# Shared expert of a decoder layer on one NeuronCore: split fp32r products with the weights stationary, two tiles of tokens at a time

## What is computed

```python
x = x + attention(layernorm(x))              # 32 heads, 8 kv heads, rope, sinks
x = x + cross_attention(layernorm(x), ctx)   # 8 heads
x = x + ffn(layernorm(x))

def ffn(h):                                  # 8 experts, top 1, 512 inner units
    logits = h @ router_w.T
    xr = h * sigmoid(logits of the chosen expert, -inf elsewhere)
    routed = (up * silu(gate)) @ down_proj[expert]
    shared = silu(h @ shared_gate_w) * (h @ shared_up_w) @ shared_down_w
    return shared + routed
```

## Time and profile before

| what | value |
|---|---|
| median of 3 runs | 2001.04 us (1997.6 to 2002.55) |
| the profiled execution's own time | 1998.05 us |
| its span in the profile | 1996.2 us |
| attention, about | to 954 us |
| cross-attention and router, about | 960 to 1554 us |
| first gate matmul of the shared tiles | 1557.25 us |
| first gate matmul of the routed tiles | 1750.52 us |
| mean granted clock of TensorE, share of full speed | 0.959 |

### The profile page before, as it was taken

One profiled execution on the slowest core, in us unless ns is written; L12 is line 12 of the kernel. 1 busy time (PEld: TensorE's weight loads), 2 busy tenths in 40 slices (PEclk: granted clock), 3 DMA queues, 4 the chain that ended last, 5 costly groups with the idle time before them and its releaser, 6 DMA issues. The chain is left out here.

```text
span 1996.2 us, 44689 instructions
## 1 busy us (share of the span) xinstructions
PE 1806.2 (90%) x14992; PEld 1378.2 (69%) x14993; DVE 1156.6 (58%) x2205; ACT 797.6 (40%) x1495; POOL 809.3 (41%) x1280
## 2 busy tenths in 40 slices
PE   3999999999999999998699999999996799999997
PEld 2777777877787778776576776676773456666664
DVE  5776677666766676765666666676772222222222
ACT  3333443344333434343266666666663111111111
POOL 3545455545554555443323333333333100034443
PEclk9999999999999999998688989999997899999999
DMA  5011111111111111112333433443431282222221
GB/s 174 16 52 54 42 43 47 53 47 41 43 53 50 42 39 53 53 35 56 102 93 87 106 98 106 106 106 101 108 96 56 76 296 71 66 66 67 64 67 39
DMA packets 142007, 148.33 MB, mean 74 GB/s; under 512 B 26962, under 2 KB 136598, under 8 KB 140154
## 3 DMA queue, kind: packets, MB, share of 16 engines
q1 hardware_dynamic: 136186, 133.46, 24.0%
q0 software_dynamic: 5760, 14.06, 2.2%
HBM read 93.46 MB, written 54.11 MB: 74 GB/s over the span
## 5 line engine op out<-in xcount | busy, mean ns | idle before, releaser
L1129 DVE TENSOR_REDUCE xmax<-bankX 128x4 f32<-128x1024 f32 x256 | 310.1, 1217 | 155.2 <-PE bankX L1214 153.6
L1084 ACT ACTIVATE xe<-bankXT 128x512 f32<-128x512 f32 x512 | 293.2, 597 | 128.6 <-PE bankXT L1225 113.9
L1225 PE MATMUL bankXT<-stq,stk 98*128 98x256 f32 x1024 | 236.7, 319 | 31.8 <-DMA stq<-sh 26.3
L369 POOL TENSOR_TENSOR roped<-ropeC,ropeD 128x512 f32<-128x512 f32 x160 | 205.8, 1292 | 57.1 <-DVE ropeD L530 57.1
L1225 PEld LDWEIGHTS bankXT<-stq,stk 98*128 98x128 f32 x1024 | 163.8, 201 | 70.0 <-ACT xe L1084 47.5
L557 DVE TENSOR_TENSOR oTl<-bankV,oTh 128x512 fp32r<-128x512 f32 x128 | 88.1, 688 | 199.4 <-ACT oTh L445 199.4
L1540 DVE TENSOR_TENSOR hid<-bankU,gate 128x512 f32<-128x512 f32 x72 | 49.8, 692 | 246.3 <-PE bankU L1593 240.0
L1214 PE MATMUL bankX<-stk,stq 96*128 96x256 f32 x1024 | 179.2, 301 | 13.7 <-DMA rw<-in_rw 11.1
L662 PE MATMUL bankQ<-wqh,xnTh 128*128 128x512 f32 x384 | 189.5, 493 | 0.0
L1486 ACT ACTIVATE gate<-bankG 128x512 f32<-128x512 f32 x72 | 43.0, 597 | 347.0 <-PE bankG L1593 347.0
L1214 PEld LDWEIGHTS bankX<-stk,stq 96*128 96x128 f32 x1024 | 153.0, 206 | 16.8 <-DMA rw<-in_rw 11.3
(11 more groups left out here) (175 smaller groups left out, 3755.0 us busy)
## 6 DMA issues: line engine op xcount, KB each, us to landing
stackk_d<-chl SPq DMA_DIRECT2D x96, 128.0 KB, 2.3
stackq_d<-q2hl SPq DMA_DIRECT2D x96, 128.0 KB, 2.3
stk<-stackk_d SPq DMA_DIRECT2D x32, 384.0 KB
stq<-stackq_d SPq DMA_DIRECT2D x128, 96.0 KB
wexp<-in_wexp SPq DMA_DIRECT2D x8, 1536.0 KB, 8.4
x_d<-x SPq DMA_DIRECT2D x64, 128.0 KB, 1.8
xrden<-inv_d SPq DMA_DIRECT2D x64, 128.0 KB, 2.5
xin<-xg_d SPq DMA_DIRECT2D x40, 128.5 KB, 2.1
```

The costliest lines, as they stand in the source:

```text
L369: nc.gpsimd.tensor_tensor(roped[c % 3][:], ropeC[c % 2][:], ropeD[c % 2][:], ALU.add).then_inc(s_rsum, 1)
L1084: nc.scalar.activation(xe[q][:].rearrange("p n m -> p (n m)"), bT[:, q % 2, :], ACT.Exp).then_inc(s_xe, 1)
L1129: nc.vector.tensor_reduce(xmax[tile[1] % 2][:, :, a:b + 1:b - a].rearrange("p m h -> p h m"), bS[:, 2 * (pr % 2):2 * (pr % 2) + 2, :].rear ...
L1225: ins = nc.tensor.matmul(bT[:, q % 2, n * D:(n + 1) * D], stk[p][0:98, hd // 4, n * P:(n + 1) * P], stq[p][0:98, hd, :], start=True, stop= ...
```

## The change

The shared expert becomes a pipeline of its own, ahead of the routed tiles. It runs over 16 groups of two tiles (256 tokens, `g`) and, in each, 4 units of 128 inner units (`n` counts all 64).

- `up_s`: 128 columns of the gate (or up) weights are stationary, `[128 features, 128 inner units]`, and the 256 tokens move; the result has the inner units on partitions. Every product is three fp32r products of the high and low parts, so 6 matmuls of 256 columns for gate and 6 for up.
- ScalarE applies silu to the gate, VectorE multiplies, ScalarE copies the high part `hsh`, VectorE subtracts to `hsl`. No transposes and no `hT` copy remain.
- `down_s`: `hsh` and `hsl` of 128 tokens are stationary, 256 columns of down weights move, 6 matmuls per unit.
- The rows must come in turned. The router's stage has them turned already (xn3T), so `cross` now stores xn3T (`xn3T_d`, 512 bytes in a row) in place of xn3. SP's store of x2 moves up behind `s_x2`, the wait for `s_norm` goes, the store of xn3T stands at the end of the tile's queue, and `xa` now waits for `s_f3` also. The ScalarE copy to xn3T waits for the store of the tile before.
- The shared weights are split once, by GpSimd in tiles 1 to 3 of `cross`, from `wraw` into `wshh` and `wshl`.
- The rows of a group are split as they arrive: ScalarE copies `xsh`, GpSimd subtracts `xsl`.
- The base row x2 is loaded, added to and stored for two tiles at a time (`xb`).
- SP loads one expert's weights in each of groups 1 to 8. The table goes out and in again in group 3.
- The routed pipeline starts when the last shared unit is through.

```diff
-                    sp.wait_ge(s_norm, at(y) + 1)
-                    sp.dma_start(G.xn3_d[bass.ds(at(y) * P, P), :], xn3[yp][:]).then_inc(s_fst[yp], 16)
+                    sp.wait_ge(s_x2, at(y) + 1)
                     sp.dma_start(G.x2_d[bass.ds(at(y) * P, P), :], x2[yp][:]).then_inc(s_fst[yp], 16)
...
+                    if five:
+                        sp.wait_ge(s_f3, at(y) + 1)
...
+                if five:
+                    if not three:
+                        sp.wait_ge(s_f3, at(y) + 1)
+                    sp.dma_start(G.xn3T_d[:, :, bass.ds(at(y) * P, P)].rearrange("k p n -> p k n"), xn3T[:]).then_inc(s_fst[y[1] % 2], 16)
...
-            sp.dma_start(G.wsh[:], A["wexp"][E]).then_inc(G.s_wsh, 16)
+            sp.dma_start(wraw[:], A["wexp"][E]).then_inc(G.s_wsh, 16)
...
+            def split_shared(i):
+                a, b = i * WE // 3, (i + 1) * WE // 3
+                if i == 0:
+                    pool.wait_ge(G.s_wsh, 16)
+                nc.gpsimd.tensor_copy(G.wshh[:, a:b], wraw[:, a:b]).then_inc(G.s_wshh, 1)
+                pool.wait_ge(G.s_wshh, 2 * i + 1)
+                nc.gpsimd.tensor_tensor(G.wshl[:, a:b], wraw[:, a:b], G.wshh[:, a:b].bitcast(F32),
+                                        ALU.subtract).then_inc(G.s_wshh, 1)
...
+                if not inside(tile) and 1 <= at(tile) < 4:
+                    split_shared(at(tile) - 1)
...
+                        o = prev(y, 1)
+                        need(act, s_fst[o[1] % 2], (pair(o) + 1) * 32)
...
+            def load_x(g):
+                need(sp, s_u, NF * (g - 1))
+                sp.dma_start(xs[g % 2][:], G.xn3T_d[:, :, g * 2 * P:(g + 1) * 2 * P].rearrange(
+                    "k p n -> p k n")).then_inc(s_xin[g % 2], 16)
+            def load_base(g):
+                need(sp, s_yst[g % 2], 16 * (g // 2))
+                sp.dma_start(xb[g % 2][:], x2_d[g * 2 * P:(g + 1) * 2 * P, :].rearrange(
+                    "(i p) d -> p i d", i=2)).then_inc(s_x2in[g % 2], 16)
+            def store(g):
+                sp.wait_ge(s_y, 2 * (g + 1))
+                sp.dma_start(base_d[g * 2 * P:(g + 1) * 2 * P, :].rearrange("(i p) d -> p i d", i=2),
+                             xb[g % 2][:]).then_inc(s_yst[g % 2], 16)
...
+            for g in range(2):
+                load_x(g)
+            for g in range(2):
+                load_base(g)
+            for g in range(1, NG + 1):
+                if 2 <= g + 1 < NG:
+                    load_x(g + 1)
+                store(g - 1)
+                if 2 <= g + 1 < NG:
+                    load_base(g + 1)
+                if g <= E:
+                    sp.dma_start(wexp[:, (g - 1) * WE:g * WE], A["wexp"][g - 1]).then_inc(s_w, 16)
...
+            def low_x(g):
+                pool.wait_ge(s_xsh, g + 1)
+                nc.gpsimd.tensor_tensor(xsl[g % 2][:], xs[g % 2][:], xsh[g % 2][:].bitcast(F32),
+                                        ALU.subtract).then_inc(s_xT, 1)
...
+            def high_x(g):
+                act.wait_ge(s_xin[g % 2], 16 * (g // 2 + 1))
+                nc.scalar.activation(xsh[g % 2][:], xs[g % 2][:], ACT.Copy).then_inc(s_xsh, 1)
+            def gate_s(n):
+                act.wait_ge(s_g, n + 1)
+                need(act, s_d, n - 1)
+                nc.scalar.activation(hs[n % 2][:], bk[n % 2][:, 0, 0:2 * P], ACT.Silu).then_inc(s_silu, 1)
+            def high_h(n):
+                act.wait_ge(s_h, n + 1)
+                nc.scalar.activation(hsh[n % 2][:], hs[n % 2][:], ACT.Copy).then_inc(s_th, 1)
...
+            high_x(0)
+            high_x(1)
+            for n in range(NS):
+                gate_s(n)
+                high_h(n)
+                if n % NF == 0 and 2 <= n // NF + 1 < NG:
+                    high_x(n // NF + 1)
...
+            def hidden_s(n):
+                dve.wait_ge(s_silu, n + 1)
+                dve.wait_ge(s_u, n + 1)
+                nc.vector.tensor_tensor(hs[n % 2][:], bS[:, n % 2, 0:2 * P], hs[n % 2][:], ALU.mult).then_inc(s_h, 1)
+            def low_h(n):
+                dve.wait_ge(s_th, n + 1)
+                nc.vector.tensor_tensor(hsl[n % 2][:], hs[n % 2][:], hsh[n % 2][:].bitcast(F32),
+                                        ALU.subtract).then_inc(s_hT, 1)
+            def result_s(g):
+                dve.wait_ge(s_d, NF * (g + 1))
+                dve.wait_ge(s_x2in[g % 2], 16 * (g // 2 + 1))
+                for i in range(2):
+                    nc.vector.tensor_tensor(xb[g % 2][:, i, :], xb[g % 2][:, i, :], bX[:, g % 2, i * D:(i + 1) * D],
+                                            ALU.add).then_inc(s_y, 1)
...
+            result_s(NG - 1)
...
+            def three(a, b):
+                return ((a[0], b[0]), (a[0], b[1]), (a[1], b[0]))
+            def up_s(n, half, out, done):
+                g, c = n // NF, n % NF
+                if half == 0:
+                    if c == 0:
+                        pe.wait_ge(s_xT, g + 1)
+                    need(pe, s_silu, n - 1)
+                else:
+                    need(pe, s_h, n - 1)
+                for k in range(2):
+                    at = (k * 2 + half) * FF + c * P
+                    for i, (w, x) in enumerate(three((wshh[:, at:at + P], wshl[:, at:at + P]),
+                                                     (xsh[g % 2][:, k, :], xsl[g % 2][:, k, :]))):
+                        ins = nc.tensor.matmul(out, w, x, start=(k == 0 and i == 0), stop=(k == 1 and i == 2))
+                ins.then_inc(done, 1)
+            def down_s(n):
+                g, c = n // NF, n % NF
+                pe.wait_ge(s_hT, n + 1)
+                if c == 0:
+                    need(pe, s_y, 2 * (g - 1))
+                at = 4 * FF + c * D
+                for j in range(2):
+                    for i, (x, w) in enumerate(three((hsh[n % 2][:, j * P:(j + 1) * P],
+                                                      hsl[n % 2][:, j * P:(j + 1) * P]),
+                                                     (wshh[:, at:at + D], wshl[:, at:at + D]))):
+                        ins = nc.tensor.matmul(bX[:, g % 2, j * D:(j + 1) * D], x, w, start=(c == 0 and j == 0 and i == 0),
+                                               stop=(c == NF - 1 and i == 2), skip_group_check=True)
+                ins.then_inc(s_d, 1)
...
+                up_s(n, 0, bk[n % 2][:, 0, 0:2 * P], s_g)
+                up_s(n, 1, bS[:, n % 2, 0:2 * P], s_u)
+                if n >= 1:
+                    down_s(n - 1)
             turn_in((0, 0))
-            seq(pe, body, EDGES)
+            down_s(NS - 1)
+            pe.wait_ge(s_tab, 16)
```

More of the change, by code:

```diff
@@ L76, in constants @@
     put("none", NTOK)
-    put("tile", p[:, None] - NTOK // P)
+    put("tile", p[:, None])
     return c
@@ L1344, in experts @@
         xin = [sb(f"xin{p}", [P, D + 1]) for p in range(2)]
+        xs = [sb(f"xs{p}", [P, 2, 2 * P]) for p in range(2)]
+        xsl = [sb(f"xsl{p}", [P, 2, 2 * P], F32R) for p in range(2)]
+        xsh = [sb(f"xsh{p}", [P, 2, 2 * P], F32R) for p in range(2)]
+        hs = [sb(f"hs{p}", [P, 2 * P]) for p in range(2)]
+        hsl = [sb(f"hsl{p}", [P, 2 * P], F32R) for p in range(2)]
+        hsh = [sb(f"hsh{p}", [P, 2 * P], F32R) for p in range(2)]
+        xb = [sb(f"xb{p}", [P, 2, D]) for p in range(2)]
         xT = [sb(f"xT{p}", [P, 2, P]) for p in range(2)]
@@ L1378, in _ @@
         def _(sp):
-            def row(tile):
-                return sp.value_load(tabr[0:1, bass.ds(num(tile) * 2, 1)], min_val=0, max_val=XROWS - P)
-            def load(tile, like):
-                h, p = tile
-                if like < NT + 2:
-                    need(sp, s_tx, num(tile) - 1)
-                else:
-                    sp.wait_ge(s_tok, num(tile) - NT - 1)
-                if like < NT:
-                    sp.dma_start(xin[p][:, 0:D], xn3_d[bass.ds(num(tile) * P, P), :]).then_inc(s_xin[p], 16)
-                else:
-                    if like == NT:
-                        sp.wait_ge(s_tab, 16)
-                        sp.wait_ge(s_padd, 16 * E)
-                        for q in range(2):
-                            sp.wait_ge(G.s_scat[q], 16 * (NT // 2))
-                    sp.dma_start(xin[p][:], xg_d[bass.ds(row(tile), P), :]).then_inc(s_xin[p], 16)
@@ new lines, in load_base, with load @@
+            def load_base(g):
[6 more added lines that the diff above has]
+                             xb[g % 2][:]).then_inc(s_yst[g % 2], 16)
+            def load(tile):
+                need(sp, s_tok, num(tile) - 1)
+                row = sp.value_load(tabr[0:1, bass.ds(num(tile) * 2, 1)], min_val=0, max_val=XROWS - P)
+                sp.dma_start(xin[tile[1]][:], xg_d[bass.ds(row, P), :]).then_inc(s_xin[tile[1]], 16)
@@ new lines, in body @@
+            def body(tile, n):
+                if n + 2 < NRT:
+                    load((tile[0] + 1, tile[1]))
+            for g in range(2):
[10 more added lines that the diff above has]
```

(28 more changed lines are left out.)

148 lines of the change are left out of this document (67 added, 81 removed).

## The result

The changed kernel takes 1930.86 us (median of 4 runs, 1925.14 to 1934.92) against 2001.8 us for the kernel before in the same session (4 runs, 1997.6 to 2005.36). The profiled execution took 1931.86 us with a span of 1930.0.

What follows compares the result with a forecast made beforehand. TensorE was taken to bound the kernel. Terms -51.4 + 1.3 + 18 + 2 + 2.8 - 14 = -41.3 us against the profiled 1998.05 us gave 1956.8; with the median 3.0 us higher, 1959 us was forecast, range 1936 to 1990.

Steps and rivals of the forecast that it cites:

- What bounds the kernel: Whole kernel: TensorE is the busy engine; the experts' stage is priced by what TensorE must stream.
- Matmuls of the shared expert: Shared stage: 64 units of 18 matmuls at 0.117 us take 134.8 us instead of 186.2, -51.4 us.
- The chain keeps up: Shared stage: a unit's chain of 1.8 to 1.9 us fits in TensorE's 2.1 us; nothing charged except in first units.
- The start: Experts' stage, first load to first gate matmul: 4.6 us instead of 3.3, +1.3 us.
- Waits for transfers in the shared stage: Groups 1 to 8 get rows late behind weights, plus the table and first units: +18 us, the least certain term.
- -51.4 + 18 + 2 + 2.8: Shared-stage terms: matmuls -51.4, transfer waits +18, clock falling at the table's wait +2, passing from shared to routed +2.8 us.
- the table: Group 3: SP waits for the table's store to land, so the next rows go out late; 7 us.
- Cross-attention: -14 us: SP issues `stq<-sh` about 0.6 us earlier in tiles 4 to 30: 13 us, plus 1 us for the last tiles.
- rival 5: Shared stage: waits bring TensorE's clock to the lower level and keep it there, up to 2070 us; chance 0.04.
- Rival 1: Shared stage: transfers stay hidden, waits 4 us instead of 22, and the clock stays up, 1939 us; chance 0.20.
- Rival 3: Cross-attention: another wait, exponentials or maxima, takes back the gain, +14 us, 1973 us; chance 0.15.
- What would show it: Signs: first routed gate matmul 42 us earlier, lengthened early groups, `stq<-sh` waits near 10 us; late groups above 8.6 us refute.

Runs made afterwards that it cites:

- b5: The change with one of the three products of each split pair left out in the shared expert, 12 matmuls per unit: 1913.85 us, ratio 0.9601.
- b1: The change with ScalarE's high-part copy of the next group's rows after a group's third unit instead of its first: 1923.08 us, ratio 0.9648.
- b2: The change with the tile table fetched back in group 10, not right behind its store in group 3: 1924.77 us, ratio 0.9665.
- a5: The change with `stq<-sh` and the loads of the inverses issued ahead of x2's store in cross-attention: 1912.12 us, ratio 0.9599.
- a3: The change with one extra, unread store ahead of `stq<-sh` on SP's queue, without the old wait: 1965.41 us, ratio 0.9866.
- a7: The change with two extra, unread stores ahead of `stq<-sh` on SP's queue: 2003.19 us, ratio 1.0032.
- a1: The change with the old wait for `s_norm` and an extra, unread store ahead of `stq<-sh`: 1973.87 us, ratio 0.9909.
- c2: The change with the edits of a5, b1 and b2 together, and `stq<-sh` also ahead of the store of the inverses: 1946.24 us, ratio 0.9742.
- d1: a7 with five matmuls, result unread, ahead of TensorE's wait for `stq<-sh`: 1969.46 us, ratio 0.9901.
- d2: a3 with five matmuls, result unread, ahead of TensorE's wait for `stq<-sh`: 1940.83 us, ratio 0.9732.
- a2: The change with only the old wait for `s_norm` put back ahead of `stq<-sh`, no extra store: 1930.73 us, ratio 0.9689.

## Why the prediction was wrong

**What bounds the kernel: right.** TensorE in every stage, and SP's queue as what it waits for in cross-attention.

**Matmuls of the shared expert: right within 3 us.** A unit takes 2.16 us and not 2.11, since a matmul's pace is 0.120 us and not 0.117: 64 units x 0.05 = 3 us. (The 109 ns that the prediction took from the Trainium skill, page "TensorE: Matmul & The Clock Gate", section "Back-to-back issue gap", was further off; the section gives that formula for single isolated matmuls, not for a stream of loads and matmuls.)

**The chain keeps up: right.** Estimated 1.8 to 1.9 us; the traces of b5 and of the change show 1.7.

**The start:** 1.8 us more instead of 1.3.

**Waits for transfers in the shared stage: right in sum and in mechanism, wrong in their parts.** The terms from first to first gate matmul were -51.4 + 18 + 2 + 2.8 = -28.6, and -28.9 came. b1 took 10.4 us of them away. But the table, priced at 7, is worth 1.4 (b2), and 10.2 us at the lower clock, in 3 spells, cost some 5 where 2 were given. The price of a group's wait also rests on a slip: weights issued at 7.1 us that take 6.6 hold the queues until 13.7 us, not 12.7, which by the prediction's own steps makes the rows 3.4 us late and not 2.4. The agreement of the sum owes much to luck.

**Cross-attention: -14 us. This is the step that failed.** It came to -38.4. What the prediction did with SP's queue was right: one store of 0.5 us in 27 tiles, and 14.8 us less waiting for `stq<-sh`. It then took the wait's length for its price, with all 26.3 us as the bound. The price is that and the clock that falls for it: 68.3 - 13.7 = 54.6 us less at half speed, worth 27 us. 14.8 + 27 = 42, against 38.4 measured. How far the sum of the two terms carries is seen over the table: take a5 and add the difference in waits and half the difference in low clock. For a3 that gives 1498.9 + 23.6 + 23.9 = 1546.4 (measured 1548.5), for a7 1594.8 (1589.2), for a1 1548.5 (1552.0), for the change 1512.9 (1520.7). The largest miss of this kind is 11 us (b1, 1510.7 against 1521.7). Three kernels fall outside: c2 ends 19 us later than so computed, for its waits are others than `stq<-sh`, and d1 and d2 end 30 us later, of which the filling itself, 0.85 us in each of 32 tiles, is 27. So it is an estimate to some 10 us. The waits for `posx` are in all of them (12.5 to 16.5 us in the loop).

The row that should have given it away was in the prediction's own groups: a clock of 0.92 in the very loop whose waits were being shortened. It was read there only as a danger (rival 5) and only for the shared stage, never as a gain to be had where waits go. The Trainium skill, page "TensorE: Matmul & The Clock Gate", section "HAM oscillation — how this bites in real kernels", says that recurring waits between bursts of matmuls keep the clock falling. The prediction held that rule against the change; d1 and d2 agree with it, with waits of only about 1 us once in a tile, but it spoke for the change. Rival 5 also says that the trace of before agrees at the table; it doesn't, the clock is at the lower level until 1563 us, in the stage's start, and at 1.00 from 1575 to 1592, while the table goes out.

**Rivals.** None of them happened. Rival 1 (1939) has the time closest to the result, for a reason that is not the one: the shared stage's waits were there. Rival 3, that another wait takes back cross-attention's gain, is what c2 did and the change did not.

**What would show it:** the lengthened groups, the named waits and the fall to about 10 us (11.5) were there. The first routed gate matmul came 65 us earlier and not 42, a tile got shorter by 1.3 us and not by 0.5 to 0.6, and late groups took 8.64 us against a limit of 8.6, all for the reasons above. The granted clock of the shared stage was 0.95, at its limit.

## What to carry to other kernels

Before pricing a wait of TensorE, look at the granted clock of that stretch: where it is below 1.00, a wait's price is its length and about half of the time at the lower clock that goes with it. Here the end of cross-attention moved by 1.9 times (a3 against a2), 2.6 times (the change) and 3.8 times (a7 against a3) what the waits did. On a DMA queue that feeds TensorE, put what TensorE needs first and stores that nobody is waiting for last, and fill with other issues the time in which the queue must see its own write land; then look again at what the move made late. On an in-order engine a wait for a transfer should stand as far behind the transfer's issue, and behind the work that TensorE needs next, as its own reader allows.

## What was unexpected of the hardware

- With a wait of about 1 us once in a tile of some 17 us (26.3 us in 30 waits in a3 and before, 37.1 in 29 in a7) the loop spent 51, 68 and 126 us at the lower clock, in 13, 15 and 20 spells; with 11.5 us in 22 (0.5 us each) it was 13.7, in 3.
- Five matmuls that nobody reads, in such a wait, made the kernel 1.3% faster.
- One more store of 0.49 us on SP's queue per tile cost 35 us, a second 33 to 38, while the store itself and what it writes are needed by nobody: 13 us of SP's time each.
- A 256-column fp32r matmul with a new stationary operand each has a pace of 0.120 us in the shared expert and 0.117 in attention. What makes the difference was not tried.
